# Attention phase of a two-layer token tower: the turn of the next group's row maxima moved from key-tile block 13 to block 14 of 0 to 15

## The reference

```
q = _rope(_heads(x @ Wq)) * DH ** (-0.5)        # 8 images x 12 heads, 1030 x 16
kv = _rope(_heads(x @ Wkv))
...
attn_lat = jax.nn.softmax(jnp.einsum('bid,bkd->bik', q_lat, kv), axis=-1)
attn_ctx = jax.nn.softmax(jnp.einsum('bid,bkd->bik', q_ctx, kv_ctx), axis=-1)
out_lat = _merge(jnp.einsum('bik,bkd->bid', attn_lat, lkv), b) @ Wo_lat + bo_lat
out_ctx = _merge(jnp.einsum('bik,bkd->bid', attn_ctx, lkv_ctx), b) @ Wo_ctx + bo_ctx
```

## Time and profile before

| | us |
|---|---|
| median of 3 runs | 5092.34 |
| those runs | 5072.34, 5092.34, 5094.30 |
| the profiled execution | 5079.84 |
| its span on the core | 5077.9 |
| TensorE busy in the span | 4304.7 (85%) |
| the 24 groups' blocks, from the span's start | 2546.9 to about 3750 |

### The profile page before, as it was taken

One profiled execution on the slowest core, in us unless ns is written; L12 is line 12 of the kernel. 1 busy time (PEld: TensorE's weight loads), 2 busy tenths in 40 slices (PEclk: granted clock), 3 DMA queues, 4 the chain that ended last, 5 costly groups with the idle time before them and its releaser, 6 DMA issues. The chain is left out here.

```text
span 5077.9 us, 71492 instructions
## 1 busy us (share of the span) xinstructions
PE 4304.7 (85%) x23656; PEld 2544.6 (50%) x23658; DVE 2617.8 (52%) x4342; ACT 1418.8 (28%) x2730; POOL 1181.5 (23%) x1317
## 2 busy tenths in 40 slices
PE   7799977769999999556599999999958588799997
PEld 7566655546666666333133333333327466566664
DVE  1466536972222222377687787777825444332332
ACT  0111111001111111122177777777741111011110
POOL 0000001013333443243300000000013100277775
PEclk9899988779999999777599999999987699899998
DMA  7111111122222232223432323232239211355554
GB/s 184 42 45 40 30 42 36 28 60 54 54 54 54 57 66 45 68 94 112 96 60 44 65 43 64 44 65 44 48 95 238 63 38 37 77 108 114 109 108 112
DMA packets 353482, 360.10 MB, mean 71 GB/s; under 512 B 66563, under 2 KB 310998, under 8 KB 353170
## 3 DMA queue, kind: packets, MB, share of 16 engines
q1 hardware_dynamic: 263106, 263.09, 22.2%
q0 software_dynamic: 62560, 74.40, 8.4%
q10 hardware_dynamic: 27632, 20.14, 1.4%
HBM read 237.14 MB, written 126.09 MB: 72 GB/s over the span
## 5 line engine op out<-in xcount | busy, mean ns | idle before, releaser
L1832 DVE TENSOR_REDUCE at_mx<-psum 128x1 f32<-128x998 f32 (+1 forms) x768 | 886.4, 1192 | 257.3 <-PE psum L1654 256.8
L1783 ACT ACTIVATE at_p<-psum 128x512 f32<-128x512 f32 (+3 forms) x1536 | 850.4, 588 | 300.7 <-PE psum L1727 272.2
L1727 PE MATMUL psum<-at_q,at_k 99*128 99x512 bf16 (+3 forms) x1536 | 522.5, 383 | 24.5 <-issue 16.8
L1654 PE MATMUL psum<-at_k,at_q 96*128 96x512 bf16 (+3 forms) x1536 | 475.6, 392 | 76.0 <-DMA at_k<-qk_parts 38.6
L1713 PE MATMUL psum<-at_p,at_v 128*32 128x486 f32 (+3 forms) x3072 | 407.3, 603 | 1.0 <-ACT at_p L1783 0.7
L1727 PEld LDWEIGHTS psum<-at_q,at_k 99*128 99x128 bf16 (+1 forms) x1536 | 155.5, 102 | 430.6 <-ACT at_p L1783 268.4
L1117 ACT ACTIVATE ex_silu<-psum 128x384 f32<-128x384 f32 (+1 forms) x288 | 131.5, 457 | 833.8 <-PE psum L1061 703.5
L1146 DVE TENSOR_TENSOR ex_hT<-ex_silu,psum 128x384 f32<-128x384 f32 (+1 forms) x288 | 147.5, 512 | 416.2 <-ACT ex_silu L1117 270.9
L1082 PE MATMUL psum<-ex_wd,ex_hT 128*128 128x192 f32 (+1 forms) x1728 | 305.3, 341 | 0.0
L1634 POOL DMA_DIRECT2D o_parts<-at_o x24 | 12.9, 539 | 1246.3 <-DVE at_mx L1832 947.0
L1082 PEld LDWEIGHTS psum<-ex_wd,ex_hT 128*128 128x128 f32 (+1 forms) x1728 | 283.6, 189 | 15.9 <-issue 3.6
(11 more groups left out here) (341 smaller groups left out, 6770.4 us busy)
## 6 DMA issues: line engine op xcount, KB each, us to landing
qk_parts<-hd_parts SPq DMA_DIRECT2D x8, 2317.5 KB
at_k<-qk_parts SPq DMA_DIRECT2D x144, 128.8 KB
at_q<-qk_parts SPq DMA_DIRECT2D x144, 124.8 KB
tok_p<-in_x SPq DMA_DIRECT2D x24, 588.0 KB
o_parts<-at_o POOLq DMA_DIRECT2D x24, 515.0 KB
pr_op<-o_parts SPq DMA_DIRECT2D x8, 1545.0 KB
pr_recip<-recips SPq DMA_DIRECT2D x32, 386.2 KB
v_rows<-hd_v_out SPq DMA_DIRECT2D x8, 1536.0 KB
```

The source lines that it names most:

```text
L1654: mm = pe.matmul(psum[0:ctx_rows[t], 3 + 2 * ((PRO + n) % 2) + k, 0:w], Q[v][0:R6, j * 1024 + 128 * t:j * 1024 + 128 * t + ctx_rows[t]], K ...
L1727: pe.matmul(psum[0:n, (u * ST_N + i) % RING, 0:w], K[u][:, j, 128 * t:128 * t + n], Q[u][:, j * 1024 + at:j * 1024 + at + w], start=True, ...
L1783: act.activation(P[0:n, c % 2, j, 0:w], psum[0:n, (u * ST_N + i) % RING, 0:w], ACT.Exp) \
L1832: dve.tensor_reduce(mx[0:ctx_rows[t], j * CT + t:j * CT + t + 1], pair(n)[0:ctx_rows[t], 0:CTX], AX_X, ALU.max).then_inc(s_free, 1)
```

## The change

One number changes. The transpose, the copy and the three DMAs of group g+1's maxima are placed in block 14 rather than block 13. `number` moves all waits with them, and no instruction is added or dropped.

```diff
-    LAT_OUT, LAT_MAX, TURN = 9, 11, 13
+    LAT_OUT, LAT_MAX, TURN = 9, 11, 14
```

## The result

| | before | after |
|---|---|---|
| median of 15 runs, us | 5079.92 | 5097.60 |
| lowest and highest | 5072.34, 5094.30 | 5088.63, 5119.43 |
| profiled execution | 5079.84 | 5104.06 |

The ratio of the runs is 1.0036, 95% interval [1.0025, 1.0047]: slower by 0.36%, within the 0.5% that the forecast called no change, and on the side that it named. The forecast was 1.0037 (18.8 us on 5086.1), in time 5105 for a measured 5097.6. Of the 7 us between them 6 come from the level of the kernel before, whose median over more runs (5079.92) is lower than the middle of the four known then.

The account below looks back on a forecast made before the run. TensorE was taken as the bound, busy 47.47 of 48.99 us in an undisturbed group. Terms 3.3 + 13.8 + 1.7 = 18.8 us, set on 5086.1, gave 5105 us (+0.37%), range 5088 to 5126.

Parts of the forecast that it names:

- The bound: Undisturbed group: TensorE busy 47.47 of 48.99 us, so its waits cost what they last; other engines' waits cost nothing until reaching it.
- job 14b: Block 14's `by_query` job needing 14a's banks: waits 0.15 us for VectorE's reductions in 22 groups, 3.3 us.
- The landing: When the third of the maxima's DMAs has landed, counted from the copy's start: +4.0 us, range 3.4 to 4.5.
- The distance: From the copy to the next group's first score: 5.94 us before, 3.20 after the change if nothing waits.
- 16 x 0.86 = 13.8: TensorE's wait for the DMAs before 16 undisturbed groups, 4.06 - 3.20 = 0.86 us each, 13.8 us together.
- Group 23: Start behind group 22's shorter blocks: distance falls from 4.7 to 2.35 us, so TensorE waits 1.7 us.
- Loop edges: Six group starts with 16.8 us of TensorE idle already: new wait hidden there, 0 us; without cover 5.2 us.
- the two on the edges: Rivals: both short edges tip into long ones, 5115 us, chance 0.12; or long edges become short, 5084 us, chance 0.06.
- the rule of the Trainium skill: Rival: clock falls behind every new wait before a group, 17 starts x 4.45 = 76 us more, 5181 us, chance 0.04.

Follow-up runs that it names:

- t15: The turn (transpose, copy, three DMAs) in block 15, nothing else, against the kernel before with it in block 13: ratio 1.0281 [1.0263, 1.0300].
- t14_one: Turn in block 14 as in the change, but the three rows sent in one DMA instead of three, against the kernel before: ratio 1.0008 [0.9997, 1.0019].
- t14_unroll: The change (turn in block 14) with TensorE's loop over groups written out, no branch back, against the kernel before: ratio 1.0012 [1.0001, 1.0023].
- t13_pool: Kernel before, turn still in block 13, with splitting the maxima into three bf16 parts moved from VectorE to GpSimd: ratio 0.9994 [0.9981, 1.0006].

## Why the prediction was right, step by step

- **The bound.** A wait of TensorE costs what it lasts: a group takes 0.88 us more, and 0.55 of idle time, 0.16 of overlap and 0.16 for job 14b are 0.87. In `t15` the long waits cost what they lasted and the fall of the clock on top.
- **The landing.** Taken at +4.0 us between 3.4 and 4.7. The first score now stands 4.04 after the copy, so with the 0.06 that it starts later the landing is at +4.0 or a little less. The three DMAs issued one after the other are what makes it so late, as `t14_one` shows by leaving two away. The landing is not a constant, though: three undisturbed starts of the profile after waited longer than the rest (1.13, 0.72 and 0.73 us), and two of `t14_unroll` 2.30 and 2.35, which puts the landing at some 5.8 us, above the upper bound of 4.7. Why was not tried. The fixed cost of 2.0 us that the forecast took from the Trainium skill, "DMA: Bandwidth & Descriptors", section "Anatomy of one DMA — SWDGE (gpsimd) path", is stated there for DMAs that GpSimd issues; these are SyncE's. As a sum it fits (1.9 + 2.0 = 3.9), but its split does not: 1.5 of the 2 us lie before the last byte (issue at +1.9, bytes to +3.4), and only some 0.5 behind it.
- **The distance.** 3.20 us expected without a wait. `t14_one` has the same order of jobs and no wait, and its distance is 3001.78 - 2998.44 = 3.34. That is 0.14 more, so a typical wait was shorter by as much: 0.71 us for an expected 0.86. The mis-sized step is the start of the copy, which I put 0.04 behind the end of VectorE's reductions, 0.46 behind the transpose. It started 0.08 before their end (3007.33 against 3007.41), 0.33 behind the transpose. The term 16 x 0.86 = 13.8 was really 12.5 us: 9.8 of idle time and 2.7 of lost overlap, less 1.6 for group 23, plus 1.6 that the loop edges gave back. That is 0.78 a start and not 0.71, because of the three late landings.
- **Job 14b.** 0.15 us expected, 0.16 measured, in 22 groups: 3.5 us for 3.3. `t14_one` isolates it.
- **Group 23.** 1.7 us of wait expected; it came with 1.40 of idle time and 0.16 of overlap. What I had not expected is that the clock halved behind it, though the idle time is short: the timeline in front of group 23 and the window behind, then the same start in `t14_unroll`, where the same 1.40 us left the clock at 1.00.

```profile
3724.40 0.41 PE L1727 MATMUL psum<-at_q,at_k 99*102 99x486 bf16 x1
3726.21 1.46 PE L1727 MATMUL psum<-at_q,at_k 99*128 99x512 bf16 x3 [1.40 <-DMA at_q<-at_mt]
```

```profile
3726.21:3736.21 10.00, 9.74 (x38) 1.75 (x38) 0.00 (x0) 6.49 (x13) 0.53 (x1) 0.66 0.13 53
```

```profile
3704.06 0.82 PE L1727 MATMUL psum<-at_q,at_k 99*128 99x512 bf16 x3 [1.40 <-DMA at_q<-at_mt]
```

```profile
3704.06:3714.06 10.00, 9.02 (x50) 2.00 (x50) 0.00 (x0) 8.69 (x17) 0.53 (x1) 1.00 0.13 53
```

  Group 23 took 43.17 us to its last values instead of 41.0 (the rows of 3726.21 and 3769.38 against 3708.0 and 3749.03): 2.1 us more.
- **Loop edges.** 0 us expected. The profile now puts three of the six to the DMAs, the rows below, and three to "issue" (8.0 us). Together that is 2.69 + 2.31 + 2.23 + 8.0 = 15.2 us, for 16.8 before: the edges' idle time did not grow. Whether the DMAs or the branch ended last in those three is not settled. That the edges hide the wait is borne out by the six starts in `t14_unroll` and by the 15.8 us in `t14_one`. What the edges did to the clock was not foreseen: the 2.4 us of the section on the result.

```profile
2755.97 0.39 PE L1727 MATMUL psum<-at_q,at_k 99*128 99x512 bf16 x1 [2.69 <-DMA at_q<-at_mt]
...
3063.00 0.39 PE L1727 MATMUL psum<-at_q,at_k 99*128 99x512 bf16 x1 [2.31 <-DMA at_q<-at_mt]
...
3374.05 0.39 PE L1727 MATMUL psum<-at_q,at_k 99*128 99x512 bf16 x1 [2.23 <-DMA at_q<-at_mt]
```

- **The rivals.** Neither of the two on the edges came true as a whole; each did at one edge. The two short ones became longer (2.76 and 2.79 us, 2.30 and 2.35 before), and behind the second of them the clock fell, which it had not before. Of the four that had been followed by half clock one no longer was (2.42 us at 3528.93, 2.96 at 3510.17 before). The clock did not fall behind any of the 16 waits in front of undisturbed groups, of 0.43 to 1.13 us. The forecast held that by the rule of the Trainium skill, "TensorE: Matmul & The Clock Gate", section "HAM oscillation — how this bites in real kernels", it would. That reads too much into the page: the kernel that it tells of waited 3 to 5 us for its DMAs. With waits of that length it came true here as well: in `t15` TensorE waited 3.3 us for a DMA before each group and ran at half clock for a time behind each, which more than doubled the price of the wait (3.9 us on top of 3.5).

The sum of the terms in the profile is 12.5 + 3.5 + 1.6 - 1.6 = 16.0 us, and the attention grew by 15.7; the forecast said 18.8, and the medians of 15 runs 17.7. The mechanism and its terms are borne out, with the wait sized a little too high. That the totals agree so closely is partly luck: the sum has no term for the clock, which gave back 2.4 us behind the edges and took 2.1 in group 23.

## What to carry to other kernels

A step that is off the critical path has a distance to its first user and a latency until it is usable; read both, in the same unit and from the same instruction, and the cost of moving it is what the latency exceeds the distance by. Where the latency is a row of DMAs issued one behind the other, joining them buys more than any place in the order: one DMA instead of three gave back all of the wait in front of the undisturbed groups. And a wait of the bound engine should be priced with what follows it: at 0.6 us it cost itself, at 3.3 us it cost itself and 3 to 5 us of half clock.

## What the runs showed of the hardware

- A branch back of TensorE's loop cost 2.2 to 3.1 us of idle time, and written out it cost nothing; ScalarE's was hidden behind TensorE's until that was gone.
- The length of the idle time alone does not decide whether the clock falls to half. No fall: 0.55 us in front of groups, 2.30 at an edge, 2.76 and 2.93 at single starts, 3.11 at an edge of `t13_pool` (2746.59). A fall: 1.40 in front of group 23, the 2.23, 2.31 and 2.69 of the three edges above, 2.79, 3.06, and the 3.33 us of `t15`. In `t14_one` one edge of 2.23 us (2746.62) was followed by half clock and one of 2.24 us (3515.45) was not. The two starts with 2.76 and 2.79, both at loop edges of the profile after, and the 20 us behind each:

```profile
2911.59 0.39 PE L1727 MATMUL psum<-at_q,at_k 99*128 99x512 bf16 x1 [2.76 <-issue]
...
3218.22 0.60 PE L1727 MATMUL psum<-at_q,at_k 99*128 99x512 bf16 x1 [2.79 <-issue]
```

```profile
2911.60:2931.60 20.00, 20.00 (x114) 6.29 (x115) 15.11 (x14) 16.14 (x29) 0.53 (x1) 1.00 0.72 125
3218.20:3238.20 20.00, 19.98 (x89) 5.56 (x93) 11.71 (x11) 12.80 (x23) 0.53 (x1) 0.76 0.75 125
```

  What tells them apart stays open; no run here was made to find it.
- Four small operations of GpSimd (0.25 us each) took the place of three of VectorE's beside the running reductions without slowing these: three of them took 3.40 us (2985.51 in `t13_pool`), as in rows 2.
